# A counter of landed gather groups for TensorE, in three gather stages of a four-layer graph network

## The reference

```python
dst = min(int(3125 * uniform(100000) ** 2), 49999)     # sorted; low nodes have the most edges
# layer 2, twice: relational convolution
H = einsum('ni,rio->nro', x, W)
agg = segment_sum(H[src, etypes] * edge_weight, dst)
# layer 4
e = relu(bn(edge_attr @ w1 + b1)) @ w2 + b2
h = h + segment_sum(e, dst)
z = h + segment_sum(h[src], dst)                       # then two dense layers with batch norm
```

## Time and profile before

| | us |
|---|---|
| median of 3 runs | 7439.35 |
| span of the profiled execution, first to last instruction | 5778.8 |
| median less span, what lies around the traced instructions | 1660.55 |
| gathers of s1: first and last start | 1285.4, 2284.8 |
| gathers of s2: first and last start | 2370.4, 3348.5 |
| gathers of s5: first and last start | 4727.8, 5711.7 |

### The profile page before, as it was taken

One profiled execution on the slowest core, in us unless ns is written; L12 is line 12 of the kernel. 1 busy time (PEld: TensorE's weight loads), 2 busy tenths in 40 slices (PEclk: granted clock), 3 DMA queues, 4 the chain that ended last, 5 costly groups with the idle time before them and its releaser, 6 DMA issues. The chain is left out here.

```text
span 5778.8 us, 72791 instructions
## 1 busy us (share of the span) xinstructions
PE 3412.2 (59%) x18712; PEld 3084.7 (53%) x18712; DVE 2595.6 (45%) x8699; ACT 1457.5 (25%) x3506; POOL 3969.2 (69%) x4127
## 2 busy tenths in 40 slices
PE   3777777755433334777777776666676653333334
PEld 3676777634333333577777765566565543333333
DVE  4666656662222222433333356777777661111112
ACT  2222222210000000333333335665666410000002
POOL 6777777607777776577777727777777527777774
PEclk6555555576665565877777788999999875555556
DMA  4333333332222211422222226555666412222111
GB/s 126 107 105 109 108 107 107 82 121 87 62 63 64 61 53 49 139 60 60 60 60 60 60 78 168 160 158 158 159 159 159 109 38 53 53 53 53 53 53 41
DMA packets 392271, 522.01 MB, mean 90 GB/s; under 512 B 105994, under 2 KB 275937, under 8 KB 391513
## 3 DMA queue, kind: packets, MB, share of 16 engines
q0 software_dynamic: 131200, 271.80, 18.9%
q1 hardware_dynamic: 258009, 245.43, 14.0%
q10 hardware_dynamic: 2689, 0.36, 0.0%
HBM read 473.25 MB, written 50.76 MB: 91 GB/s over the span
## 5 line engine op out<-in xcount | busy, mean ns | idle before, releaser
L1047 PE MATMUL PS<-arena,att 128*128 x3328 | 735.4, 412 | 1219.5 <-DMA arena<-tab_h,HT 615.8
L1047 PEld LDWEIGHTS PS<-arena,att 128*128 128x128 f32 x3328 | 685.3, 315 | 1271.3 <-issue 1271.2
L1510 POOL DMA_INDIRECT arena<-tab_x,idx_a x880 | 831.4, 945 | 314.1 <-issue 265.5
L993 POOL DMA_INDIRECT arena<-tab_rel,idx_b x782 | 762.3, 975 | 397.3 <-issue 238.0
L679 POOL DMA_INDIRECT arena<-tab,idx_a x832 | 819.1, 984 | 259.4 <-issue 252.0
L993 POOL DMA_INDIRECT arena<-tab_h,HT x782 | 746.9, 955 | 300.5 <-issue 238.0
L491 POOL DMA_INDIRECT arena<-tab_rel,idx_b x782 | 741.0, 948 | 275.0 <-issue 238.0
L1024 DVE TENSOR_SCALAR att<-iota_row,drel 128x128 f32<-128x128 f32 x832 | 182.0, 307 | 814.5 <-PE PS L1047 814.4
L1020 DVE TENSOR_SCALAR att<-iota_row,drel,wgt 128x128 f32<-128x128 f32 x832 | 222.3, 364 | 694.3 <-PE PS L1047 694.2
L583 DVE TENSOR_TENSOR arena<-arena,PS 128x128 f32 x832 | 240.5, 289 | 598.8 <-PE PS L547 524.1
L543 PE MATMUL PS<-arena,att 128*128 x1664 | 368.3, 362 | 228.8 <-DMA arena<-tab_rel,idx_b 206.2
(11 more groups left out here) (374 smaller groups left out, 5252.6 us busy)
## 6 DMA issues: line engine op xcount, KB each, us to landing
arena<-pair_d SPq DMA_DIRECT2D x220, 256.0 KB
arena<-tab_u SPq DMA_DIRECT2D x880, 64.0 KB
arena<-drel_rows SPq DMA_DIRECT2D x104, 512.0 KB
tab_rel<-arena SPq DMA_DIRECT2D x50, 512.0 KB
arena<-tab_rel,idx_b POOLq DMA_INDIRECT x1564, 2.5
arena<-tab_x,idx_a POOLq DMA_INDIRECT x880
arena<-tab,idx_a POOLq DMA_INDIRECT x832
arena<-tab_h,HT POOLq DMA_INDIRECT x782
```

Of the source, the lines that this page charges most:

```text
L993: pool.indirect_dma_start(out=G[:, o:o + D], out_offset=None, in_=table, in_offset=bass.IndirectOffsetOnAxis(ap=src[:, c:c + 1], axis=0)). ...
L1047: ins = nc.tensor.matmul(acc, M[s % RM][:, k * P:(k + 1) * P], G[:, bass.ds(e * (2 * D) + g * D, D)], start=False, stop=True, skip_group_c ...
L1510: pool.indirect_dma_start(out=G[:, o:o + D], out_offset=None, in_=tab_x, in_offset=bass.IndirectOffsetOnAxis(ap=idx_pair[:, 4 * g + u:4 * ...
```

## The change

A second semaphore, `landed`, counts groups that have landed, in order. GpSimd raises it: behind the third gather of group g it waits for group g-1's `full` and adds 1, and behind the last gather it does the same for the last group. VectorE works out, once per stage, which group the last step of each set uses: `estep[4s+3] >> 2`, plus 1. TensorE loads that number for set s into a register and waits for `landed` to reach it, in place of the wait for group s. The new wait stands in all 104 sets.

```diff
--- before.py
+++ after.py
@@ -44,6 +44,7 @@
 PC, PB = 8, 110
 PR = PC * PB
 assert NB + TN - 1 <= PR and PR % 4 == 0
+GATHERS = -(-ST // 4)
 FAR, FLOOR = 2.0 ** 60, 2.0 ** 58
 NW = NT * D
 ARENA = 30720
@@ -136,6 +137,17 @@
             _, values = nc.values_load_multi_w_load_instructions(row[0:1, bass.ds(at, 4)], engines=[eng], min_val=0, max_val=top,
                 skip_runtime_bounds_check_because="every tile number and step is clamped to this range on chip, where it is computed")
             return values
+
+        def needed_groups(dve, row, done):
+
+            dve.tensor_scalar(row, estep[:, 3::4], 2, None, ALU.arith_shift_right).then_inc(done, 1)
+            dve.wait_ge(done, 1)
+            dve.tensor_scalar(row, row, 1, None, ALU.add).then_inc(done, 1)
+
+        def load_need(eng, row, s):
+
+            return nc.values_load(row[0:1, s:s + 1], engines=[eng], min_val=1, max_val=GATHERS)
+
 
         class Chain:
 
@@ -465,8 +477,9 @@
             GE = A[:, o:o + NQ * 1024]
             assert o + NQ * 1024 <= ARENA
             M, MW = ([att[:, 2048 * j + 1024 * i:2048 * j + 1024 * (i + 1)] for i in range(2)] for j in range(2))
-            pos = HT[0:1, 0:SS].bitcast(I32)
+            pos, need = HT[0:1, 0:SS].bitcast(I32), HT[0:1, SS:SS + SETS].bitcast(I32)
             full = [sem(f"s2_g{q}") for q in range(RG)]
+            landed = sem("s2_landed")
             attr_full = [sem(f"s2_at{q}") for q in range(NQ)]
             m_done, w_done, sum_done, add_done, z_done, r_done, s_ones, s_pos = (
                 sem("s2_" + x) for x in ("m", "w", "s", "a", "z", "r", "one", "pos"))
@@ -492,6 +505,12 @@
                                 out=G[:, o:o + D], out_offset=None, in_=table,
                                 in_offset=bass.IndirectOffsetOnAxis(ap=idx_row[:, c:c + 1], axis=0)
                             ).then_inc(full[g % RG], 16)
+                            if g and c == 8 * g + 2:
+                                pool.wait_ge(full[(g - 1) % RG], 128 * ((g - 1) // RG + 1))
+                                pool.sem_inc(landed, 1)
+                    last = GROUPS_N - 1
+                    pool.wait_ge(full[last % RG], 128 * (last // RG) + 16 * (2 * ST - 8 * last))
+                    pool.sem_inc(landed, 1)
 
                 @block.scalar
                 def _(act):
@@ -525,15 +544,15 @@
                         ins.then_inc(z_done, 1)
 
                     features(0)
-                    pe.wait_ge(s_pos, 1)
+                    pe.wait_ge(s_pos, 3)
                     for s in range(SETS):
                         if s + 1 < SETS:
                             features(s + 1)
                         at = load_tiles(mybir.EngineType.PE, pos, s * 4, 4 * RG - 1)
+                        groups = load_need(mybir.EngineType.PE, need, s)
                         pe.wait_ge(r_done, s + 1)
                         pe.wait_ge(w_done, s + 1)
-                        if s < GROUPS_N:
-                            pe.wait_ge(full[s % RG], 128 * (s // RG) + 16 * min(8, 2 * ST - 8 * s))
+                        pe.wait_ge(landed, groups)
                         for u, e in enumerate(at):
                             if s:
                                 pe.wait_ge(add_done, 2 * (4 * s + u - 3))
@@ -555,6 +574,7 @@
                     for y in Y:
                         ch(dve.memset(y[:, :, D:WY], 1.0))
                     dve.sem_inc(s_ones, 1)
+                    needed_groups(dve, need, s_pos)
                     dve.tensor_scalar(pos, estep[:], 4 * RG - 1, None, ALU.bitwise_and).then_inc(s_pos, 1)
                     ch(dve.memset(ACC, 0.0))
 
@@ -962,6 +982,8 @@
             pos = HT[0:1, 2368:2368 + SS].bitcast(I32)
             zeros = A[:, 30208:30720]
             full = [sem(f"{name}_g{q}") for q in range(RG)]
+            need = HT[0:1, 2840:2840 + SETS].bitcast(I32)
+            landed = sem(name + "_landed")
             s_ix, s_rows, s_pos = sem(name + "_ix"), sem(name + "_rows"), sem(name + "_pos")
             m_done, sum_done, s_zero = sem(name + "_m"), sem(name + "_s"), sem(name + "_z")
             with nc.Block() as block:
```

## The result

| | median us | lowest to highest | runs |
|---|---|---|---|
| changed kernel | 7458.33 | 7431.53 to 7478.48 | 12 |
| kernel before, same chip | 7439.51 | 7418.63 to 7453.22 | 12 |

The ratio is 1.0028 (95% 1.0015 to 1.0040): 19 to 21 us slower, small but measured. The forecast was 7447, no measurable change; the time lies in its range. The profile shows that most of the working behind that number doesn't describe the timed runs.

What follows compares the result with a forecast made beforehand. GpSimd issuing gathers, with TensorE's tail behind, was taken as the bound. -52.8 + 30.6 + 5.8 + 23.5 + 0.5 = +7.6 us on the median gave 7447, no measurable change; low end 7415, high end 7485.

Steps and rivals of the forecast that it cites:

- Step 1: Ends of s1, s2, s5: the late sets start before the last gather lands; gains 12.9, 27.0, 12.9, together -52.8 us.
- Step 2: Start of s1: GpSimd waits for delayed first landings before gathers 11 and 19; +30.6 us, never regained.
- Set 41's +5.8: Near set 41 in s1: the plan's transposing DMAs delay a landing GpSimd now waits for; +5.8 us, between 0 and 9.
- Step 3: GpSimd's queue, all three stages: 294 raises between gathers at 0.08 us each, +23.5 us.
- rival C: Faster: raises on GpSimd cost nothing or little, start costs 25 to 30; 7423, or 7412 us; chance 0.20.
- Step 4: TensorE's queue: one more register load per set, hidden by running products or idle time except for late sets; +0.5 us.
- if that cover fails: Three late sets of each stage on TensorE: register loads no longer hidden, 9 x 0.4 = 3.6 us.
- rival B: Slower: each raise holds GpSimd longer, 0.158 us giving 7470, a full gap of 0.305 giving 7513; chance 0.27.

Runs made afterwards that it cites:

- last sets alone: Against the kernel before, only sets from 92 on load and use the counter, GpSimd raising from group 80 on: 7433.79 against 7434.10 us, 1.0001.
- the two with two queues: SyncE and ScalarE each issue half of s1's slot copies: kernel before so edited 7286.94 us, changed kernel so edited 7314.21 us.
- the loads alone: Kernel before plus one unused register load of the needed group per set on TensorE, no raises: 7465.46 against 7453.83 us, 1.0011.

## Why the prediction came out near

**What bounds the kernel: wrong, and the step that failed.** The forecast landed near by luck. The prediction read "bound by GpSimd issuing gathers" from a profile of 5778.8 us and added the result to a median of 7439.35, "taking the 1660.55 us outside the span as unchanged". Those 1660 us are inside the span of the timed executions, 875 of them in the three stages as delays of TensorE's and SyncE's queues, the rest in other stages and not traced to a cause. The page's numbers for before and the median could not both belong to one state of the machine; that gap, 22% of the time, was the thing to weigh, with a rival of its own. Everything below follows from it.

**Step 1, the tails, -52.8: wrong in the timed runs.** TensorE doesn't wait for the last gather; it has a backlog of a dozen sets. Starting the last sets early gains nothing (last sets alone: -0.3 us). The tails of s1 and s5 grew instead, by 9 to 10 us each where one chip has both kernels (the two with two queues). On a chip of the faster kind, where the seven waiting sets are there, the step may hold; the changed kernel wasn't run on one.

**Step 2, the start of s1, +30.6: right as a stall, wrong as a price.** 24.0 + 5.25 = 29.2 us of gaps stand where they were forecast, 28.6 above the usual. "Nothing gives the 30.6 back" failed: GpSimd's first wait for a free buffer is 12 to 13 us shorter, and SyncE's copies, not the sums, end the stage. Net about 11 us. Set 41's +5.8 is one gap of 0.76 us in place of 0.30 in the changed kernel (before gather 411, in group 51), and of 2.34 and 3.25 us in two others (before gather 403).

**Step 3, the raises, +23.5: wrong, they are free.** The gap is 0.305 with and without wait and raise. This was rival C's price. The Trainium skill (Advanced Engine Details and Errata, "Engine Queue Depths" and "Sequencer Loop") says that GpSimd has a queue of 8 and that other instructions can be read and queued while one executes. The traces agree with it: one more instruction in the queue leaves the gap at 0.305. I had set the constant gap against it, but that gap doesn't tell whether the queue works ahead.

**Step 4, TensorE's loads, +0.5: mis-sized, and the wrong way round.** The prediction gave "if that cover fails" 9 x 0.4 = 3.6. The cover fails for each set of a backlog: 0.65 us x about 13 sets = 8.5 us in s1 and in s5, an estimate that the two-queue runs meet (9.6 and 8.7) and the loads alone meet in s1 (7.6) but not in s5 (2.1). In all the loads alone cost 8 to 12 us, and five of them 88.

So +7.6 was the sum of a gain that isn't there, a true stall at nearly three times its net price, a cost that isn't there, and a cost put at next to nothing. By its own mark of 0.2% (15 us) "no measurable change" was missed: 19 to 21 us is on rival B's side of the line, and for another reason than B's. The measured +19 is, by the experiments, about 11 for the start and, as what is left, about 8 for the loads.

## What to carry over

Before pricing anything, make the profiled span and the median agree; if they don't, the profile shows another machine than the runs, and its bound may not be theirs. A register load per loop turn is free only while its engine waits for others: price it at the backlog's pace too (here 0.65 us a set). And look at which queue ends a stage: a row of small DMA issues that looks finished early in one profile was worth 175 us in the runs.

## What the hardware showed that I had not expected

- Two kinds of chip for one program: medians of 7434 to 7462 us on some, 5791 on one in one session (a factor of 1.28 to 1.29), the runs of each within 0.3% of their median. On the slow kind TensorE's, SyncE's and ScalarE's queues step by 0.70 and 1.40 us in the stages of GpSimd's gathers, also in its pauses; GpSimd's own pace (0.95 us and a gap of 0.305) and VectorE's masks (0.34 us in the median of s1) are the same on both.
- What differs between the chips is open. The number of gathers matters (782 to 98 in s5: 444 slow steps to 4), the program's length alone doesn't.
- A wait and a raise between two indirect DMAs on GpSimd add nothing that shows (median gap 0.305 with and without), as long as the wait is met.
- SyncE's copies take 5.2 us each beside the gathers and 1.6 us behind them.
